# Causal groups and window attention written out straight, unpadded value rows, and the causal mask moved from TensorE to VectorE

## The reference, cut to what matters

```python
xn = _layernorm(x)                                  # x: (4, 1024, 256)
# causal attention, 16 heads of 16 columns
Q, K, V = proj(W_q), proj(W_k), proj(W_v)
scores = einsum('bhqd,bhkd->bhqk', Q, K) * 16 ** -0.5
scores = where(causal, scores, -inf)
s = (softmax(scores) @ V) @ W_o.T
# two layers on xn: window attention (8 heads of 64, windows of 128 rows
# that also see the window before), then a gated feed-forward of 682 columns
for l in range(2):
    xn = xn + local_attention(rotary(l2norm(q)), rotary(l2norm(k)), v) @ wo[l]
    h = layernorm(shift_token(xn)) * lg + lb
    a, g = split(h @ w1 + b1)
    xn = xn + (a * gelu(g)) @ w2 + b2
out = x + s * silu(xn)
```

## Time and profile before

| | |
|---|---|
| median of 3 runs | 2124.43 us (2120.41 to 2127.48) |
| the profiled execution | 2127.53 us, its span 2125.7 us |
| busy: PE, PEld, DVE, ACT, POOL | 1902.0, 1376.4, 1504.3, 1208.7, 961.0 us |
| projection | 0 to about 138 us |
| causal attention | about 138 to 693 us |
| layer 1: windows, feed-forward | about 693 to 1142, to about 1365 us |
| layer 2: windows, feed-forward | to about 1828, to about 2050 us |
| output | to 2125.7 us |

### The profile page before, as it was taken

The page is one execution under the profiler, slowest core; times in us unless marked ns, Lnnn a source line. Parts: engine busy times, 40 slices in busy tenths (PEclk is TensorE's granted clock), DMA queues, the critical chain, the costliest instruction groups (busy, mean ns, idle before and its releaser), DMA issues. The chain is left out here.

```text
span 2125.7 us, 44153 instructions
## 1 busy us (share of the span) xinstructions
PE 1902.0 (89%) x13472; PEld 1376.4 (65%) x13472; DVE 1504.3 (71%) x3610; ACT 1208.7 (57%) x2501; POOL 961.0 (45%) x789
## 2 busy tenths in 40 slices
PE   5769999999997699999996999779999999699976
PEld 4633433343442588888885788668888887578865
DVE  5657778786882598989995554269898999555424
ACT  3314656565666477777774434257777777443323
POOL 3441112121121677777771433267777777143320
PEclk9868999999999799999997999879999999799988
DMA  5791645645540100000022121200000002212137
GB/s 203 270 213 27 90 66 72 87 68 74 78 62 21 47 28 28 26 25 25 25 68 65 30 59 50 93 13 25 25 25 25 25 26 69 62 30 59 51 117 244
DMA packets 165019, 143.35 MB, mean 67 GB/s; under 512 B 31298, under 2 KB 145406, under 8 KB 164734
## 3 DMA queue, kind: packets, MB, share of 16 engines
q1 hardware_dynamic: 163518, 140.14, 28.0%
q10 hardware_dynamic: 1344, 1.31, 0.2%
HBM read 90.80 MB, written 50.35 MB: 66 GB/s over the span
## 5 line engine op out<-in xcount | busy, mean ns | idle before, releaser
L654 DVE TENSOR_REDUCE ca_mx<-ca_pR 128x1 f32<-128x512 f32 (+3 forms) x768 | 375.8, 549 | 90.8 <-PE ca_pR L524 47.8
L631 ACT ACTIVATE ca_pr<-ca_pS 128x1024 f32<-128x1024 f32 (+3 forms) x384 | 300.4, 813 | 242.8 <-PE ca_pS L548 184.0
L811 POOL TENSOR_TENSOR w_tsn<-w_qk,w_tab 128x512 f32<-128x512 f32 x128 | 260.2, 2052 | 188.6 <-DVE w_pn L1009 171.9
L888 ACT ACTIVATE w_pe<-w_sm,w_nmax 128x256 f32<-128x256 f32 x512 | 253.3, 497 | 151.3 <-DVE w_nmax L1000 151.3
L463 POOL TENSOR_SCALAR_AFFINE_SELECT ca_pr<-ca_pr 128x256 f32<-128x256 f32 x256 | 103.9, 406 | 429.3 <-ACT ca_pr L631 427.0
L521 PE MATMUL ca_pR<-ca_ks,ca_qs 96*128 96x512 bf16 (+3 forms) x768 | 240.7, 350 | 18.9 <-DVEq L707 16.3
L1000 DVE CUSTOM_DVE_ANT_0 w_sm<-w_pS,masks 128x256 f32<-128x256 f32 x512 | 185.9, 420 | 31.9 <-PE w_pS L1184 19.4
L548 PE MATMUL ca_pS<-ca_qs,ca_ks 98*128 98x512 bf16 (+3 forms) x768 | 191.6, 333 | 15.1 <-issue 13.1
L521 PEld LDWEIGHTS ca_pR<-ca_ks,ca_qs 96*128 96x128 bf16 x768 | 73.4, 99 | 186.5 <-DVE ca_mx L654 125.4
L819 POOL TENSOR_TENSOR w_rs<-w_ssc,mhalf 128x16 f32<-128x16 f32 x64 | 187.5, 2930 | 5.3
L1009 DVE TENSOR_SCALAR w_pn<-w_pe,w_rsum 128x256 f32<-128x256 f32 x512 | 182.8, 419 | 4.6
(11 more groups left out here) (163 smaller groups left out, 4416.4 us busy)
## 6 DMA issues: line engine op xcount, KB each, us to landing
QKP<-p_parts SPq DMA_DIRECT2D x32, 384.0 KB, 3.3
ca_qs<-QKP SPq DMA_DIRECT2D x96, 128.0 KB, 6.5
ca_ks<-QKP SPq DMA_DIRECT2D x96, 128.0 KB, 7.0
VA<-p_vaug SPq DMA_DIRECT2D x8, 1024.0 KB, 5.4
ca_va<-VA SPq DMA_DIRECT2D x16, 512.0 KB, 10.6
w_xt<-X SPq DMA_DIRECT2D x64, 128.0 KB, 2.0
X<-w_x SPq DMA_DIRECT2D x64, 128.0 KB, 1.7
f_hh<-X SPq DMA_DIRECT2D x32, 256.0 KB, 4.7
```

The costliest lines, as they stand in the source:

```text
L631: act.activation(pr[:, k % 2, pair, :, 0:w], pS[:, pair, :, 0:w], ACT.Exp, scale=CS).then_inc(p_ready, 1)
L654: dve.tensor_reduce(mx[:, i, h, ch:ch + 1], pR[jb % RING][:, 0:w], AX.X, ALU.max, negate=True).then_inc(ring_free, 1)
L811: pool.tensor_tensor(dst, src[:, :, ::-1, :], s, ALU.mult).then_inc(S["ts_ready"], 1)
L888: ins = act.activation(pe_[:, h], sm[:, n], ACT.Exp, bias=nmax[:, n:n + 1], scale=-1.0, accum_out=sums[:, h:h + 1])
```

## The change

- In the causal stage the loop is gone for all engines: 16 groups in a row with constants. VectorE's loop over windows is gone too; the other engines keep theirs.
- The mask matmul L524 and `mask_q` are gone. For the 32 diagonal jobs of a group VectorE runs the custom operation of L1000 instead of the reduction: it adds `later`, a 128 by 512 float tensor whose last 128 columns hold the mask, writes the sum to a scratch tensor in SBUF, and takes the negated maximum. A semaphore increment stands between its wait and the operation. The other 16 jobs keep the reduction.
- `VA` holds 16 columns for each head, arranged by batch, group and partition. A store of the projection is 512 KB in place of 1 MB, a load of a group 256 KB in place of 512 KB, with 2 KB in one piece for each partition in place of eight pieces of 512 B.
- The load goes to a new tensor `vin`. GpSimd copies it into the padded `va` (`spread`), for group n+1 after the second diagonal step of group n, and TensorE waits for it before the first `weighted` of a group. Zeros and ones are set once in `va` at the start of the causal stage, and no longer in `vaug`.

```diff
@@ stack_transfers
-    qs, ks, va, _ = K.stacks
+    qs, ks, vin, _, _ = K.stacks
-    va_t = VA.rearrange("(b t p) (g c) -> b g p t c", b=BATCH, p=P, g=CG)
-    return out + [(va[:, u], va_t[n // CG, n % CG])]
+    return out + [(vin[:, u], VA[n // CG, n % CG])]
@@ phase_project
-        va_t = VA.rearrange("(s n p) c -> s p n c", n=SUP, p=P)
+        va_t = VA.rearrange("b g p (f n) c -> b f p g n c", f=2)
-                sp.dma_start(va_t[s], vaug[:, j].rearrange("p n h w -> p n (h w)")).then_inc(v_stored[j], 16)
+                sp.dma_start(va_t[it, j], vst[:, j]).then_inc(v_stored[j], 16)
-                pool.memset(vaug[:, :, :, :, CD + 1:VW], 0.0).then_inc(v_preset, 1)
-                pool.memset(vaug[:, :, :, :, CD:CD + 1], 1.0).then_inc(v_preset, 1)
-                    dve.tensor_copy(vaug[:, j, 2 * v:2 * v + 2, :, 0:CD],
-                                    pV[:, v].rearrange("p n (h w) -> p n h w", w=CD)).then_inc(v_copied, 1)
+                    dve.tensor_copy(vst[:, j, :, 2 * v:2 * v + 2],
+                                    pV[:, v].rearrange("p n (g c) -> p g n c", g=CG)).then_inc(v_copied, 1)
@@ phase_causal, all engines
-            step(0, 0, 0, False, 2)
-            with e.Fori(0, LOOPS) as it:
-                for u in range(1, SLOTS + 1):
-                    step(it * SLOTS + u, u % SLOTS, it + u // SLOTS, True, 2)
-            for n in range(LOOPS * SLOTS + 1, ITERS):
-                step(n, n % SLOTS, n // SLOTS, True, min(ITERS - 1 - n, 2))
+            for n in range(ITERS):
+                step(n, n % SLOTS, n // SLOTS, n > 0, min(ITERS - 1 - n, 2))
@@ GpSimd
-            pool.memset(mask_q[:, :], 0.0).then_inc(made, 1)
+            pool.memset(later[:, :], 0.0).then_inc(made, 1)
+            heads = va[:, :, :, :].rearrange("p u t (h w) -> p (u t h) w", w=VW)
+            pool.memset(heads[:, :, CD + 1:VW], 0.0).then_inc(va_preset, 1)
+            pool.memset(heads[:, :, CD:CD + 1], 1.0).then_inc(va_preset, 1)
+            def spread(u, it):
+                pool.wait_ge(loaded[u % SLOTS], ONE + (it + 1 + u // SLOTS) * LOADS * 16)
+                pool.sem_inc(K.passed, 1)
+                pool.tensor_copy(va[:, u % SLOTS].rearrange("p t (h w) -> p t h w", w=VW)[:, :, :, 0:CD],
+                                 vin[:, u % SLOTS].rearrange("p t (h d) -> p t h d", d=CD)).then_inc(va_ready, 1)
+            spread(0, 0)
                 for i, k in enumerate(DIAGONAL):
+                    if i == SPREAD_AT and more:          # SPREAD_AT = 2
+                        spread(u + 1, it)
@@ TensorE
-                diag = k0 + w == (i + 1) * P
-                ins = pe.matmul(bank[:, 0:w], ..., start=True, stop=not diag)
-                if diag:
-                    ins = pe.matmul(bank[:, w - P:w], K.identb[:, :], mask_q[:, :], start=False, stop=True)
-                ins.then_inc(ring_full, 1)
+                pe.matmul(bank[:, 0:w], ..., start=True, stop=True).then_inc(ring_full, 1)
+                if k == 0:
+                    pe.wait_ge(va_preset, ONE + 2)
+                    pe.wait_ge(va_ready, ONE + n + 1)
@@ VectorE
+                if ch * 512 + w == (i + 1) * P:
+                    dve.sem_inc(K.passed, 1)
+                    dve.tensor_tensor_reduce(masked[:, jb % RING, 0:w], pR[jb % RING][:, 0:w], later[:, 512 - w:512],
+                                             -1.0, BIG, ALU.add, ALU.min, mx[:, i, h, ch:ch + 1])\
+                       .then_inc(ring_free, 1)
+                else:
                     dve.tensor_reduce(mx[:, i, h, ch:ch + 1], pR[jb % RING][:, 0:w], AX.X, ALU.max,
                                       negate=True).then_inc(ring_free, 1)
@@ phase_window, VectorE
-            with dve.Fori(0, NW // TPB - 1) as seq:
-                for t in range(TPB):
-                    step(seq * TPB + t, t % 4, seq * 2 + t // 4, t)
-            for t in range(TPB):
-                step(NW - TPB + t, t % 4, (NW - TPB + t) // 4, t)
+            for w in range(NW):
+                step(w, w % 4, w // 4, w % TPB)
```

More of the change, by code:

```diff
@@ L105, in phase_project @@
         rest = sb("p1_rest", [P, CG, SUP * P], F32)
-        vaug = sb("p1_vaug", [P, 2, SUP, CH, VW], F32)
+        vst = sb("p1_vst", [P, 2, CG, SUP, GH * CD], F32)
         pT = ps("p1_pT", [P, KD, 512], F32)
@@ L120, in phase_project @@
         part_stored = [sem(f"p1_part_stored{i}") for i in range(CG)]
-        v_ready, v_copied, v_preset = sem("p1_v_ready"), sem("p1_v_copied"), sem("p1_v_preset")
+        v_ready, v_copied = sem("p1_v_ready"), sem("p1_v_copied")
         v_stored = [sem(f"p1_v_stored{i}") for i in range(2)]
         x_t = x.rearrange("(s n p) d -> s p n d", n=SUP, p=P)
-        va_t = VA.rearrange("(s n p) c -> s p n c", n=SUP, p=P)
+        va_t = VA.rearrange("b g p (f n) c -> b f p g n c", f=2)
         block = c.enter_context(nc.Block())
@@ L163, in rest_of @@
                         for transfer in stack_transfers(K, QKP, VA, 0, 0)[g * share:(g + 1) * share]:
[L164 removed]
+                            sp.dma_start(*transfer).then_inc(K.stacks[4][0], 16)
                 sp.wait_ge(v_copied, ONE + 2 + s * 2 + 2)
[L166 removed]
+                sp.dma_start(va_t[it, j], vst[:, j]).then_inc(v_stored[j], 16)
             def step(s, j, it, final):
@@ L249, in _ @@
         def _(dve):
-            start_at_one(dve, mine + K.stacks[3])
+            start_at_one(dve, mine + K.stacks[4])
             dve.sem_inc(rest_ready, CG)
@@ L360, in phase_causal @@
     LATE_STEP = 1
+    SPREAD_AT = 2
     RJ = NJ + 3
     HALF = SEQ // 2
-    LOOPS = (ITERS - 2) // SLOTS
     def plan(started, more):
@@ L404, in sem @@
             return mine[-1]
-        qs, ks, va, loaded = K.stacks
-        mask_q = sb("ca_mask_q", [P, P], BF16)
+        qs, ks, vin, va, loaded = K.stacks
+        later = sb("ca_later", [P, 512], F32)
+        masked = sb("ca_masked", [P, RING, 512], F32)
         mx = sb("ca_mx", [P, TPB, GH, 2], F32)
@@ L424, in phase_causal @@
         s_ready, p_ready, pv_done = sem("ca_s_ready"), sem("ca_p_ready"), sem("ca_pv_done")
-        cut = sem("ca_cut")
+        cut, va_preset, va_ready = sem("ca_cut"), sem("ca_va_preset"), sem("ca_va_ready")
         ot_copied, rec_done = sem("ca_ot_copied"), sem("ca_rec_done")
@@ L434, in run @@
             first()
-            step(0, 0, 0, False, 2)
-            with e.Fori(0, LOOPS) as it:
-                for u in range(1, SLOTS + 1):
-                    step(it * SLOTS + u, u % SLOTS, it + u // SLOTS, True, 2)
-            for n in range(LOOPS * SLOTS + 1, ITERS):
-                step(n, n % SLOTS, n // SLOTS, True, min(ITERS - 1 - n, 2))
+            for n in range(ITERS):
+                step(n, n % SLOTS, n // SLOTS, n > 0, min(ITERS - 1 - n, 2))
         @block.gpsimd
         def _(pool):
-            pool.memset(mask_q[:, :], 0.0).then_inc(made, 1)
+            pool.memset(later[:, :], 0.0).then_inc(made, 1)
             pool.memset(mx[:, :, :, :], BIG).then_inc(made, 1)
             pool.wait_ge(made, ONE + 2)
-            pool.affine_select(out=mask_q[:, :], in_=mask_q[:, :], compare_op=ALU.is_ge, fill=NEG,
+            pool.affine_select(out=later[:, 512 - P:512], in_=later[:, 512 - P:512], compare_op=ALU.is_ge, fill=NEG,
                                base=0, pattern=[[-1, P]], channel_multiplier=1).then_inc(made, 1)
@@ L519, in maxima @@
                 bank = ring(*job)
-                diag = k0 + w == (i + 1) * P
-                ins = pe.matmul(bank[:, 0:w], qs[0:SHIFT_ROW, u, h, i * P:(i + 1) * P],
-                                ks[0:SHIFT_ROW, u, h, k0:k0 + w], start=True, stop=not diag)
-                if diag:
-                    ins = pe.matmul(bank[:, w - P:w], K.identb[:, :], mask_q[:, :], start=False, stop=True)
-                ins.then_inc(ring_full, 1)
+                pe.matmul(bank[:, 0:w], qs[0:SHIFT_ROW, u, h, i * P:(i + 1) * P],
+                          ks[0:SHIFT_ROW, u, h, k0:k0 + w], start=True, stop=True).then_inc(ring_full, 1)
             def load_wait(u, it):
@@ L653, in take_max @@
                 dve.wait_ge(ring_full, ONE + n * RJ + jb + 1)
-                dve.tensor_reduce(mx[:, i, h, ch:ch + 1], pR[jb % RING][:, 0:w], AX.X, ALU.max,
-                                  negate=True).then_inc(ring_free, 1)
+                if ch * 512 + w == (i + 1) * P:
[4 more added lines that the diff above has]
+                else:
+                    dve.tensor_reduce(mx[:, i, h, ch:ch + 1], pR[jb % RING][:, 0:w], AX.X, ALU.max,
+                                      negate=True).then_inc(ring_free, 1)
             def split(n, jobs_before):
@@ L1757, in program @@
         QKP = nc.dram_tensor("QKP", [BATCH * CG, P, 3, SEQ], BF16, kind="Internal").ap()
-        VA = nc.dram_tensor("VA", [TOK, CH * VW], F32, kind="Internal").ap()
+        VA = nc.dram_tensor("VA", [BATCH, CG, P, TPB, GH * CD], F32, kind="Internal").ap()
         AO = nc.dram_tensor("AO", [TOK, D], F32, kind="Internal").ap()
@@ L1809, in program @@
```

(1 more changed line is left out.)

3 lines of the change are left out of this document (removed).

## The result

The changed kernel takes 2096.59 us (median of 4 runs, 2093.29 to 2100.96) against 2124.69 us for the kernel before (4 runs, 2120.41 to 2127.48). The ratio is 0.9871, with a 95% interval of 0.9842 to 0.9899: faster by 21.5 to 33.6 us. Predicted were 2086 us and 2074 to 2107 as the range. The sign and the range held; the measured time lies 10.6 us above the predicted one and 0.6 us outside the forecast's own range (2075 to 2096).

What follows compares the result with a forecast made beforehand. In a causal group DVE was taken to set the pace up to about the 16th maximum, then PE. Terms of -14.6, -0.8, -5.2, -15.0, +0.4, -3.2 and +0.3 gave -38.1 us: 2086 us from the median, range 2074 to 2107.

Steps and rivals of the forecast that it cites:

- Loop jumps: Causal stage: the three jumps of the loop of three groups cost 14.6 us, and they go.
- Rival 1: Causal stage: straight code stalls as often as the loop, so the 14.6 us stay: 2101 us; chance 0.10.
- Window loop: Window attention: DVE's loop over windows costs 1.2 to 1.4 us at a jump, together 5.2 us saved.
- The mask's move: Causal groups: masking the maxima on DVE instead of PE gains 1.0 us net in a group, 15.0 us in fifteen.
- the one on the increment: DVE, between wait and masked operation: hidden while DVE is busy; 0.1 us lost in a group, up to 0.27 us each.
- early mask matmuls are free: Causal group: some 10 of 32 mask matmuls lie where DVE sets the pace and are worth nothing there.
- The value rows: End of the projection: 1.25 MB less to transfer gains 3.2 us, from 1 to 5.
- The spread: GpSimd's copy before the third diagonal cut: takes 1.2 us (0.4 to 2.5) and hides in POOL's idle time.
- The first distance: First two copies of the maxima: among the fifteen groups predicted to gain 1.0 us each.
- Rival 2: Causal stage: DVE is the bound almost everywhere, mask matmuls were free; 15.0 gained become 3 lost: 2104 us; chance 0.20.
- Rival 3: Masked maxima: wait and increment not hidden, each pays 0.27 us: 2193 us; decides from about 0.13 us; chance 0.05.
- Rival 4: Causal groups: less matmul work lowers PE's clock, giving 40 us back, about 2126 us, no change; chance 0.04.

Runs made afterwards that it cites:

- a: Changed kernel with the causal loop of three groups put back for all engines; 2115.49 us, ratio 0.9945.
- h: Kernel before with both loops written out and nothing else changed; 2103.37 us, ratio 0.9891.
- e: Changed kernel with VectorE's loop over windows put back; 2105.53 us, ratio 0.9906.
- i: g with 8 early diagonal jobs (row blocks 7 and 6) masked by a matmul on TensorE and reduced plainly; 2086.09 us, ratio 0.9818.
- j: g with 8 late diagonal jobs (row blocks 1 and 0) masked by a matmul on TensorE and reduced plainly; 2091.95 us, ratio 0.9840.
- b: Changed kernel with the mask matmuls back on TensorE and plain reductions for all 48 maxima on VectorE; 2098.64 us, ratio 0.9882.
- c: Changed kernel with plain reductions and no mask matmul, so the mask of the maxima is left out; 2084.52 us, ratio 0.9811.
- k: g without GpSimd's two increments between a wait and the diagonal cut or the spread; 2085.04 us, ratio 0.9812.
- g: Changed kernel without the increment before the masked operation on VectorE; 2086.95 us, ratio 0.9817.
- d: Changed kernel with the mask matmuls back on TensorE while VectorE keeps its masked operation; 2115.48 us, ratio 0.9955.
- l: Changed kernel as it is, measured and profiled again on the same chip as k; 2099.40 us, ratio 0.9874.
- f: c with only the increment put back before the plain reduction in the 32 diagonal jobs; 2091.79 us, ratio 0.9845.

## Why the prediction was right, and where its terms were off

- **Loop jumps, right.** -14.6 us predicted, all three gone, and 13.5 us come back with the loop (a). Rival 1 is false: in neither the changed kernel nor h has PE a gap of over 1.2 us in the causal stage behind the first group's start.
- **Window loop, right.** -5.2 predicted, 5.4 measured between the 2nd and 30th windows, 6.7 from the other side (e). The 3.4 us more in the first and last windows were not predicted; they go with PE's clock there, which differs between traces of the same window code.
- **The mask's move, mis-sized, and by far the largest miss.** The step that failed is the one on the increment: "When DVE has to wait for PE, it may cost up to the whole 0.27 us [...] I take little of it, 0.1 us in a group, since it falls where three banks give slack". It costs 0.76 us. The upper bound of 0.27 us a wait was safe; the assumed slack was not there. Where DVE has waited for PE it is behind for the next jobs, PE waits for a bank a few jobs further on, and so 0.15 us in DVE's start holds back every job behind it. The other two terms were near: matmuls 1.17 for 1.3, the operation 0.11 for 0.2. Net 0.30 us in a group in place of 1.0, or 14 x 0.30 = 4.2 us in place of 14. That early mask matmuls are free did not hold either (0.030 us each, i); late ones cost 0.045 and not 0.06 (j), so the two errors nearly cancelled in the 1.3.
- **The value rows, mis-sized both ways.** 3.2 us predicted at the start, 6.07 measured (h against b; 5.0 to 8.0 over all traces). The prediction saw the hold of the compute chain and the final wait, and counted one gain for both; they add up. It also took the rate of the earlier trace rows for all of the time from 105 us on. There the queues are as busy, but move 269 GB/s, and at that rate its 1.25 MB are 4.6 us (an estimate). The stretch in the kernel before:

```profile
105.00:125.00 20.00, 16.30 (x86) 14.55 (x86) 7.72 (x13) 7.94 (x13) 7.00 (x6) 0.83 1.09 269
```

The spread hides as predicted, but 0.11 us in a group, 1.5 us in 14, come back by PE's first `weighted`. The duration of the spread was taken as 1.2 us; the row says half:

```profile
172.52 0.61 POOL L455 COPY ca_va<-ca_vin 128x512 f32<-128x512 f32 x1
```

- **The first distance went the other way.** It was to shorten by 1.0 us and grew from 31.03 to 32.03. It is treated below.
- **The sum on the traces.** -38.1 predicted, -33.9 measured. In the 15 distances the causal loop gave -15.9 for -15.4 (h against before), the value rows +1.2 for 0 (b against h), and the mask's move -2.1 for -15.0 (the changed kernel against b), the first distance counted in each. The start gave -5.8 for -2.5, the windows -8.8 for -5.2, and the stretches that vary by themselves -2.4 for 0. So 12.9 us too much at the mask were hidden by some 9 us too little elsewhere, and that part of the closeness is luck. The medians moved by 28.1 only, since the two traced executions lie at opposite ends of their spreads; a forecast from one traced execution carries some 3 us of that at either end.
- **The rivals.** Rival 2, DVE as the bound everywhere, is false: with the mask matmuls away and DVE's work unchanged (c against b), the group shrinks by 1.17 us. Rival 3 had the right mechanism and the wrong price: the increment isn't hidden when DVE waits, but it is 0.15 us at five of 32 jobs, 0.024 us on average, and by the prediction's own sum it decides from 0.13. Rival 4 is false in regular groups, whose clock is 1.00.

## What to carry to other kernels

On DVE here an instruction that only passes a semaphore was free while the engine was busy, and cost 0.11 to 0.15 us where it stood behind a real wait and another engine waited for what came after it: count such waits, not the instructions. On POOL, whose work was never late, it cost nothing (k). Look at each increment between a wait and an operation and ask whether it is still needed; g computes the same as the changed kernel without it. And a gain in PE's busy time (1.3 us in a group here, of which 0.3 was left) has to be set against what the engine that receives the work does in its own waits.

## What the runs showed of the hardware that was not expected

**0.15 us for an increment behind a wait on DVE**, as shown above (0.11 before a plain reduction); none measurable on POOL (k).

**The clock of the first group.** Stretches of the changed kernel after its first copy:

```profile
169.00:173.00 4.00, 4.00 (x16) 0.98 (x14) 2.88 (x9) 1.62 (x2) 1.24 (x3) 0.50 0.00 0
173.00:175.00 2.00, 1.97 (x12) 0.79 (x8) 1.08 (x4) 0.54 (x1) 0.13 (x1) 0.70 0.00 0
175.00:177.00 2.00, 1.95 (x18) 0.73 (x16) 1.91 (x7) 1.05 (x4) 0.81 (x2) 1.00 0.00 0
```

The same of c:

```profile
160.00:166.00 6.00, 2.51 (x10) 0.88 (x8) 1.75 (x3) 1.01 (x1) 0.00 (x0) 0.50 0.01 3
166.00:168.00 2.00, 2.00 (x7) 0.65 (x6) 1.69 (x4) 1.04 (x2) 0.53 (x2) 0.63 0.00 0
```

PE waits for the turned maxima, its clock stands at 1.2 GHz, and work picks up at about 164 us. In c the clock goes to 2.4 GHz at about 167.5 us, in the changed kernel at about 174 us, though PE is busy without a break from 169. The first distance grows by more than the regular group does: against c by 3.27 us in the changed kernel (0.87 in a regular group; the clock rises 13 us after the copy, in c 7 us after it) and by 4.72 in d (1.85; 14 us). What is left, 2.4 and 2.9 us, goes with 6 and 7 us more at the low clock. Likewise the 1.00 us by which it grew over the kernel before, where the clock rises 10 us after the copy. The same working gives 0.2 to 0.4 us for each us longer at the low clock in all thirteen traces beside c. The moment belongs to the code more than to the execution: in the four traces with the same first group and its increment (the changed kernel, l, e, a) the clock rises 12.9 to 13.5 us after the copy and the distance is 32.02 to 32.04 us; in g and k it rises 13.6 us after it, and the distance is 31.08 and 31.07. It was not isolated what in the code sets it. The page "TensorE: Matmul & The Clock Gate" of the Trainium skill, Part 1, ties this clock to how busy the engine has lately been; the trace agrees in kind, and no run here shows what sets the moment.

**Open.** Why single executions of one kernel lie 7 us apart: the longer ones of the changed kernel were not traced, and l's trace, 2 us longer than the first, has the same first distance. And one distance of 31.46 us among those of 31.13 in the changed kernel: it stands at the same group in d, e and l; i and j have such a one a group later, with the next shorter by as much, and f, g and k have it at the second distance.
